# Where the softmax's probabilities are scaled: from POOL's own pass into ACT's and DVE's casts, with 16-bit scores for every second head

## The reference

```
x = x + 0.5 * ffn(layernorm(x))
x = x + attn(layernorm(x))       # 16 heads of 128, 4 kv heads, rotary, causal
x = x + 0.5 * ffn(layernorm(x))

# in attn, for each batch and head:
scores = q @ k.T / sqrt(128)     # q, k rotated; masked where j > i
attn   = softmax(scores)
out    = (attn @ v) * head_scale
y      = concat(out over heads) @ Wo
```

## Time and profile before

| | |
|---|---|
| median of 3 runs | 1106.16 us (1105.7 to 1106.87) |
| the profiled execution | 1105.64 us, span 1103.9 us |
| PE busy | 1074.5 us, 97% of the span |
| PEld busy | 847.3 us, 77% |
| DVE busy | 940.7 us, 85% |
| ACT busy | 809.1 us, 73% |
| POOL busy | 704.7 us, 64% |
| mean granted clock of TensorE | 0.991 |

### The profile page before, as it was taken

The page is one execution under the profiler, slowest core; times in us unless marked ns, Lnnn a source line. Parts: engine busy times, 40 slices in busy tenths (PEclk is TensorE's granted clock), DMA queues, the critical chain, the costliest instruction groups (busy, mean ns, idle before and its releaser), DMA issues.

```text
span 1103.9 us, 26841 instructions
## 1 busy us (share of the span) xinstructions
PE 1074.5 (97%) x8521; PEld 847.3 (77%) x8521; DVE 940.7 (85%) x2337; ACT 809.1 (73%) x2020; POOL 704.7 (64%) x876
## 2 busy tenths in 40 slices
PE   7999997899999999999999999999999998999998
PEld 4556654688888888888888888888888886566665
DVE  6798887799999999999999999999999996433433
ACT  4687986588787787877878878888787784444443
POOL 2465665477677777777777777777777773444444
PEclk9999999899999999999999999999999999999999
DMA  9432331144343344343443434334434343100101
GB/s 348 139 58 40 58 58 23 37 80 79 69 86 67 71 84 78 71 81 71 81 81 71 76 67 91 67 71 81 81 71 81 71 81 68 30 19 19 38 19 38
DMA packets 262134, 79.93 MB, mean 72 GB/s; under 512 B 249296, under 2 KB 260816, under 8 KB 261840
## 3 DMA queue, kind: packets, MB, share of 16 engines
q1 hardware_dynamic: 261664, 79.19, 34.3%
q10 hardware_dynamic: 432, 0.27, 0.1%
HBM read 12.85 MB, written 4.19 MB: 15 GB/s over the span
## 4 chain that ended last, share of the span: by engine, by line
PE 74%; issue 9%; DVE 6%; POOL 6%; ACT 4%; DMA 1%; POOLq 0%; DVEq 0%; ACTq 0%
PE bank L688 46%; PE bank L748 14%; POOL SCR L388 5%; PE bank L657 5%; PE bank L677 4%; PE bank L649 4%; ACT SCR L573 1%; DVE ARENA L1058 1%; DMA SCR<-ARENA 1%; ACT SCR L465 1%; DVE SCR L889 1%; ACT ARENA L580 1%; DVE bank L1038 1%; DVE ST L836 0%; DVE SCR L1019 0%
## 5 line engine op out<-in xcount | busy, mean ns | idle before, releaser
L414 POOL TENSOR_SCALAR SCR<-SCR,RI 128x128 f32<-128x128 f32 (+1 forms) x512 | 309.5, 604 | 44.0 <-DVE RI L1054 3.8
L399 POOL TENSOR_TENSOR SCR<-SCR 128x512 f32<-128x512 f32 x160 | 203.1, 1269 | 156.7 <-DVE SCR L1019 148.4
L573 ACT ACTIVATE SCR<-bank,NM 128x128 f32<-128x128 f32 (+1 forms) x512 | 208.6, 420 | 125.2 <-DVE NM L1038 125.2
L388 POOL TENSOR_TENSOR SCR<-SCR 128x512 f16<-128x512 f32 x128 | 152.0, 1188 | 173.7 <-ACT SCR L480 172.7
L545 ACT COPY SCR<-bank 64x512 f32<-64x512 f32 x320 | 185.6, 580 | 21.6 <-PE bank L688 15.4
L748 PE MATMUL bank<-SCR 128*128 128x128 f32 (+1 forms) x1024 | 193.7, 332 | 2.5 <-ACT SCR L573 2.5
L1058 DVE TENSOR_TENSOR ARENA<-SCR,ARENA 128x768 f16<-128x768 f32 x128 | 187.8, 1467 | 4.4 <-ACT ARENA L580 3.4
L688 PE MATMUL bank<-WOH,ARENA 128*128 128x256 f16 x1024 | 188.5, 273 | 2.2 <-DVE ARENA L1049 1.3
L889 DVE SCALAR_TENSOR_TENSOR SCR<-SCR,CS,bank 128x512 f32<-128x512 f32 x128 | 95.2, 744 | 112.0 <-PE bank L657 103.5
L1038 DVE CUSTOM_DVE_ANT_0 bank<-bank,MASK,SCQ 128x128 f32<-128x128 f32 (+1 forms) x512 | 182.9, 417 | 0.8
L488 ACT ACTIVATE SCR<-bank,SU 128x512 f32<-128x512 f32 x128 | 87.7, 685 | 117.3 <-PE bank L649 117.3
(11 more groups left out here) (115 smaller groups left out, 1654.4 us busy)
## 6 DMA issues: line engine op xcount, KB each, us to landing
out<-X SPq DMA_DIRECT2D x7, 512.0 KB, 2.9
X<-in_x SPq DMA_DIRECT2D x1, 2560.0 KB, 10.0
ARENA<-in_wq SPq DMA_DIRECT2D x1, 2048.0 KB, 13.9
ARENA<-in_wo SPq DMA_DIRECT2D x1, 2048.0 KB, 18.9
SCR<-ARENA SPq DMA_TRANSPOSE x128, 3.6
X<-in_x SPq DMA_DIRECT2D x3, 512.0 KB, 9.6
X<-in_wu SPq DMA_DIRECT2D x1, 1024.0 KB, 6.7
X<-in_wg SPq DMA_DIRECT2D x1, 1024.0 KB, 8.9
```

The source lines that it names most:

```text
L388: gp.tensor_tensor(HL[:, f % 4, :], H32[:, f % 2, :], HH[:, f % 4, :], ALU.subtract).then_inc(s["hl_done"], 1)
L399: gp.tensor_tensor(dst, M1[:, m, :], M2[:, m, :], ALU.add).then_inc(add, 1)
L414: last = gp.tensor_scalar(EX[:, par, lo:hi], EX[:, par, lo:hi], RI[:, par, c:c + 1], PS, ALU.mult, ALU.mult)
L573: last = act.activation(EX[:, par, 384 * hh + lo:384 * hh + hi], SBK[hh][:, lo:hi], ACT.Exp, bias=NM[:, par, c:c + 1], scale=-1.0, accum_o ...
```

## The change

POOL's `norm` goes. DVE multiplies the reciprocals by PS once for each pair (a new 128x4 instruction behind the reciprocal, RI0 to RI). ACT's cast of 768 columns becomes four multiplications by RI, one for each of the four column blocks (QUADS), from the unscaled EX. DVE's subtract becomes four instructions that multiply EX by RI and subtract the high half. POOL gets `halves`: after each rotated q it cuts the second head's 256 columns into QH and QL, after each k all 512 columns into KH and KL. TensorE's scores of the second head (hh = 1) become three f16 matmuls for each block instead of one in f32; the first head's stay f32.

```
+        QH, QL = pieces(2048, 2304, F16, 2), pieces(2304, 2560, F16, 2)
+        KH, KL = (sb(n, [P, 2, 512], F16) for n in ("KH", "KL"))
+        RI0 = sb("RI0", [P, 4], F32)
+        QUADS = [(384 * hh + lo, 384 * hh + hi) for hh in range(2) for lo, hi in BLOCKS]
...
+            def halves(r, full, hi, lo):
+                wait_alone(gp, add, r + 1)
+                gp.tensor_scalar(hi, full, 1.0, None, ALU.mult).then_inc(qk_hi, 1)
+                wait_alone(gp, qk_hi, r + 1)
+                gp.tensor_tensor(lo, full, hi, ALU.subtract).then_inc(qk_lo, 1)
...
-            def norm(e, par):
-                wait_alone(gp, rcp, e + 1)
-                for hh in range(2):
-                    for blk, (lo, hi) in enumerate(BLOCKS):
-                        c, lo, hi = 2 * hh + blk, 384 * hh + lo, 384 * hh + hi
-                        last = gp.tensor_scalar(EX[:, par, lo:hi], EX[:, par, lo:hi], RI[:, par, c:c + 1], PS, ALU.mult, ALU.mult)
-                last.then_inc(pn, 1)
...
                             rope_add(r - 1, 1 - m, KF[:, g, :], 8 * u - 8)
+                            halves(r - 1, KF[:, g, :], KH[:, g, :], KL[:, g, :])
...
                         rope_add(r, m, QF[:, i % 2, :], 2 * t - 2)
-                    if real(b, i, 2):
-                        norm(t - 2, i % 2)
+                        halves(r, QF[:, i % 2, SEQ:], QH[:, i % 2, :], QL[:, i % 2, :])
...
-                        act.wait_ge(pn, e + 1)
+                        act.wait_ge(rcp, e + 1)
                         wait(act, pt_t[par], 16 * (4 * b + (i - 3) // 2))
-                        act.copy(PR[:, par, 0:768], EX[:, par, :]).then_inc(p_hi, 1)
+                        for c, (lo, hi) in enumerate(QUADS):
+                            last = act.mul(PR[:, par, lo:hi], EX[:, par, lo:hi], RI[:, par, c:c + 1])
+                        last.then_inc(p_hi, 1)
...
+                    if hh == 1:
+                        pe.wait_ge(qk_lo, 5 * u + i % 4 + 2)
...
+                        else:
+                            q = [a[:, i % 2, blk * P:(blk + 1) * P] for a in (QH, QL)]
+                            k = [a[:, g, kv * SEQ:kv * SEQ + hi - lo] for a in (KH, KL)]
+                            last = pairs(bk[:, lo:hi], lambda c: q[0], lambda c: q[1], lambda c: k[0], lambda c: k[1], 1, blk == 0, blk == 1)
...
-                        wait(ve, pn, e - 1)
-                        ve.reciprocal(RI[:, par, :], RS[:, par, :]).then_inc(rcp, 1)
+                        ve.reciprocal(RI0[:, :], RS[:, par, :]).then_inc(rcp0, 1)
+                        wait_alone(ve, rcp0, e + 1)
+                        ve.tensor_scalar(RI[:, par, :], RI0[:, :], PS, None, ALU.mult).then_inc(rcp, 1)
...
-                        ve.tensor_tensor(PR[:, par, 768:1536], EX[:, par, :], PR[:, par, 0:768], ALU.subtract).then_inc(p_lo, 1)
+                        for c, (lo, hi) in enumerate(QUADS):
+                            last = ve.scalar_tensor_tensor(PR[:, par, 768 + lo:768 + hi], EX[:, par, lo:hi], RI[:, par, c:c + 1], PR[:, par, lo:hi],
+                                                           ALU.mult, ALU.subtract)
+                        last.then_inc(p_lo, 1)
```

More of the change, by code:

```diff
@@ L176, in program @@
         half_done, out_done = sem("last_sums_half_done"), sem("out_done")
[L178 to L181, removed]
+        proj, swap, mul, add, qk_hi, qk_lo, v_hi, v_lo = (
+            sem(n) for n in ("proj_done", "rope_swapped", "rope_mul", "rope_add", "qk_hi", "qk_lo", "v_hi", "v_lo"))
+        s_done, mx, ex, rcp0, rcp = (
+            sem(n) for n in ("scores_done", "max_done", "exp_done", "recip_done", "recip_scaled"))
         pt_t = [sem(f"probs_turned{i}") for i in range(2)]
@@ L747, in scores @@
                     for blk, (lo, hi) in enumerate(BLOCKS):
-                        last = pe.matmul(bk[:, lo:hi], QF[:, i % 2, hh * SEQ + blk * P:hh * SEQ + (blk + 1) * P],
-                                         KF[:, g, kv * SEQ:kv * SEQ + hi - lo], start=blk == 0, stop=blk == 1,
-                                         skip_group_check=True)
+                        if hh == 0:
+                            last = pe.matmul(bk[:, lo:hi], QF[:, i % 2, blk * P:(blk + 1) * P], KF[:, g, kv * SEQ:kv * SEQ + hi - lo],
+                                             start=blk == 0, stop=blk == 1, skip_group_check=True)
+                        else:
+                            q = [a[:, i % 2, blk * P:(blk + 1) * P] for a in (QH, QL)]
+                            k = [a[:, g, kv * SEQ:kv * SEQ + hi - lo] for a in (KH, KL)]
+                            last = pairs(bk[:, lo:hi], lambda c: q[0], lambda c: q[1], lambda c: k[0], lambda c: k[1], 1, blk == 0, blk == 1)
                     last.then_inc(s_done, 1)
```

## The result

The changed kernel took 1250.7 us (median of 4 runs, 1249.2 to 1252.1) against 1105.9 us (4 runs): a ratio of 1.131, 95% interval 1.129 to 1.132. It is 144.8 us slower. 1289 was forecast, with 1195 to 1340 as the range.

A forecast was written before the change was run, and what follows sets the result against it. TensorE and DVE were taken as full, and the change priced on the DVE-ACT ring: 6 x 1.23 + 2 x 2.17 = 11.7 us per batch, over 15.6 batches 183 us, on 1105.6 giving 1289 us; range 1195 to 1340.

The forecast's parts named there:

- the ring: The round DVE and ACT make per head pair in attention; neither has slack, low half starts 0.66 us later, at 3.99.
- ACT's four: ACT's four scaled multiplications replacing the cast of 768 columns: 1.50 us instead of 0.84, ending at 3.95.
- DVE's four: DVE's four multiply-and-subtract instructions for the low probabilities: 1.34 us undisturbed against 0.88 for the one subtract.
- ordinary pair: Head pair without k's work on POOL: DVE's four and POOL's cast and subtract take turns, 1.23 us more.
- the rule it took from them: DVE instructions with two inputs in SBUF and POOL's instructions exclude each other; a held one ends shortly after the other.
- the port: Shared SBUF access of DVE and POOL, locked for a whole instruction; forecast as taken in turns, one instruction each.
- The first pair of a unit: First head pair of each k unit, two per batch: POOL's k work delays the q add, 2.17 us more.
- The sum: Six ordinary pairs and two first pairs add 11.7 us per batch; over 15.6 batches 183 us.
- Rival 1: DVE runs its four through once it has the port and POOL waits: 6.7 us per batch, 1210 us; chance 0.22.
- Rival 2: POOL's new work costs nothing anywhere: 0.60 us more for every pair, 75 us, 1181 us; chance 0.06.
- Rival 3: TensorE sets the pace and its work falls by 20 us: 1086 us; chance 0.05 with any other no-loss way.
- Rival 4: TensorE, idle a quarter of the time, gets a lower clock; at 0.66 throughout 1436 us; chance 0.05.

The follow-up runs named there:

- experiment 1: Changed kernel without the 16-bit halves of q and k, both heads' scores in f32: 1176.1 us.
- experiment 5: Changed kernel with PS = 1 and DVE's small multiply of the reciprocals gone: 1243.8 us.
- experiment 7: Changed kernel, POOL's cast written with two multiplications by 1.0 instead of one: 1277.4 us for q alone, 1257.8 us for q and k.
- e12: Changed kernel, POOL's cast of q alone written with two multiplications by 1.0 instead of one: 1277.4 us.
- e13: Changed kernel, POOL's casts of q and k both written with two multiplications by 1.0 instead of one: 1257.8 us.
- e10: As experiment 1, with PS = 1, no small multiply, ACT's high halves before the exponentials and DVE's low halves before the rope products: 1127.7 us.

## Why the prediction was right, and where it was off

- **The bound.** Right. Two engines were full, and the change was priced on DVE and ACT, not on TensorE in whose favour the chain spoke. The loss came, and the ring closes where it was worked out: the low halves start at 3.96 (3.99 forecast).
- **ACT's four.** Right: 1.49 us (1.50 forecast), ending at 3.93 (3.95). The upper bound of 1.63 "no overlap" doesn't come out of the prediction's own prices (0.40 and 0.506 twice are 1.81); nothing hung on it.
- **DVE's four.** Right: 1.41 us undisturbed in experiment 1, and 5.30 us for its pair. DVE's small multiply was hidden in the ordinary pair as said, but not for the reason given: it isn't 0.17 us but stands 0.58 behind POOL's add. The prediction's own had the hint, a TENSOR_SCALAR of DVE with one input that POOL held, while the rule it took from them spoke of two inputs only. In the first pairs it wasn't hidden (7 us, experiment 5).
- **POOL's work in an ordinary pair.** Here the forecast was off, by 0.53 of 1.23 us. The mechanism was right, a size was not: q's cast was priced at 0.48 from the scaling, and it took 0.89. The scaling in that row has two operations, the cast has one; experiment 7 shows that this is the difference. The longer cast gave the port back after some 0.4 us all the same, and its only effect was that POOL's subtract asked too late to come between DVE's low halves. With the cast at 0.45 (e12) the subtract came in between as forecast. An error in the direction of more work made the kernel faster.
- **The first pair of a unit.** 2.15 measured, 2.17 forecast, with two errors that met: k's cast took 1.49 us instead of 0.69 and moved the q add later, and POOL's cast came only behind DVE's second low half and its subtract behind the fourth, where the forecast had them ahead of the second and the third. With k's cast at 0.62 (e13) only the second error is left, and the pair grows by 1.52. That the sum met 2.17 was luck.
- **The sum.** 9.04 per batch instead of 11.7. Six times 0.53 too much for the ordinary pairs is 3.2, and the layer norm's subtract, 0.5, was not in the sum. 141 us of 144.8 are in the batches. The casts' length is not the whole of the miss: e13, in which both have nearly the length that was priced, took 1257.8 us and not 1289. Its batch grows by 9.4, not 11.7; 1.3 of these 2.3 are the first pairs, the rest the ordinary ones, which grow by 0.86 to 1.16 there, not 1.23. The two mis-sized casts moved the time in opposite directions (q's to its true length took 27 us off, k's put 20 on), which is luck too.
- **Rival 1** (DVE runs through, 1210 us) described the ordinary pair's outcome nearly, but is refuted as a rule by e12. **Rival 2** (POOL's new work is free, 1181 us) is what experiment 1 measures, 1176, and the change is 75 above it. **Rival 3** (TensorE's 20 us) is refuted by experiment 1, in which TensorE has its old work and the time is 1176. **Rival 4** does occur, for 5 us of most batches (581 to 586 us at a granted clock of 0.66, behind 5 us with 2.49 busy), but decided nothing: the batch of 638.75 to 692.75 us stood at 1.00 and took the same 54.00 us.

The Trainium skill's lock (SBUF — State Buffer, the part on the separate sides of SBUF) agrees with what e12 shows for DVE instructions with two SBUF inputs. The same page has it for a DVE instruction in a 2-port mode as well, and the small multiply's 0.58 us, until POOL's add ended, agree with that. That the lock is held for the whole instruction doesn't fit POOL's slow cast, which held DVE for some 0.4 of its 0.89 us; there the measurement decides.

## What to carry to other kernels

Where two engines are full, read the ring that they turn in from one pair's timeline and place each new instruction in it: e10 and experiment 1 differ by 48 us in the places and one small multiply. Of work on POOL, ask first when it will ask for the port, then how long it is; a shorter instruction that comes in between DVE's can cost more than a longer one that comes behind them. And take a duration only from a row with the same operations, not from the same opcode and width.

## What the runs showed of the hardware that I had not expected

- POOL's multiply with one operation took 0.89 us for 256 columns and 1.49 for 512; with two operations (times 1.0 twice) 0.45 and 0.62, to f16 in both cases. With f32 output the one-operation form took 0.89 too.
- While that slow form ran (609.60 to 610.49), DVE instructions with two SBUF inputs were held only until about 610.0: the second low half ended at 610.32, and the third, 610.24 to 610.58, was not held at all. In e12, where POOL's cast was over at 650.50 after 0.44 us, the second low half stood just as long (0.61).
- The engines of this kernel meet at the port as well as at semaphores, and size is no protection. DVE's multiply of four columns, SBUF to SBUF, took 0.17 us at the least and 0.58 at the median, where it stood until POOL's add ended. The reciprocal of the same four columns was never held (ns min/median/max):

```profile
L1066 DVE TENSOR_SCALAR RI<-RI x128: 171/581/1257, 211.0 to 1064.2; 128x4 f32<-128x4 f32 x128
...
L1064 DVE RECIPROCAL RI<-RS x128: 156/163/178, 210.8 to 1063.9; 128x4 f32<-128x4 f32 x128
```
